# Two attentions and four experts on one core: one instruction for two heads' maxima, paired PSUM banks, rounded first layers

## The chip, the cores and the metric

The kernel runs on one core of a Trainium2 chip. The metric is the time of one execution on the device, in microseconds (us). TensorE multiplies matrices, VectorE, ScalarE and GpSimd work on vectors, SyncE starts the DMAs. Matrix results land in PSUM, eight banks of 512 float32 columns on 128 partitions; here ScalarE and VectorE empty them.

## The reference

The input x has 2048 tokens of width 128. All is float32.

```
x = x + attention1(layernorm(x))      # 16 heads of 64, position encoding added to the keys
x = x + block2(layernorm(x))
block2(s):
    a = attention2(s) @ Wo + bo       # 16 heads of 8, softmax over all 2048 keys
    x = layernorm(s + a) * g1 + b1
    key = floor(x @ router_w + router_b) mod 4
    for e in 0..3:  y_e = relu(x @ W1[e] + b1[e]) @ W2[e] + b2[e]    # 128 -> 512 -> 128
    return layernorm(x + y_key) * g2 + b2
```

Every softmax subtracts a maximum per query and head, as the kernel does too.

## The kernel before

Each engine has a program written out by hand; semaphores join them. The first attention has 32 chunks (8 pairs of heads, 4 chunks of 512 queries). A chunk has 8 double steps `j`, each with two key tiles of 128: scores on TensorE (three rounded products for each of two heads, L511), a seed with minus the maxima and an exponential on ScalarE (L842, L835), values (L533). The sums of the exponentials are added up on GpSimd and VectorE (L999, L1399, L1663).

The second attention has 16 blocks, each of 4 heads and 512 queries, of 16 steps each. A step has four score tiles of 512 columns on 32 rows of the array each (`scores2`, L639) in three banks in turn (`sc2`), four exponentials on ScalarE (`exps2`, L857), and the values (`values2`, L653, eight instructions for four heads). For a later block it also finds maxima: four matmuls (`max2`, L619) of 128 queries by 512 keys, one head each, and for each a VectorE instruction that takes the maximum of a row (`reduce_max`, L1480). TensorE's order in step T is:

```
scores2(T+1, 0); max2 of heads 2, 3; scores2(T+1, 1); values2(T)
scores2(T+2, 2); max2 of heads 0, 1; scores2(T+2, 3); items2(n, t)
```

The text calls the second line's scores and maxima group C, and those of the next step's first line, up to its values, group A. The maxima of group C are b, those of group A are a. From `MAX2_STEPS` = 11 on, a step's maxima are those of the block after next. An item (`items2`) is one further use of a bank: rows of the output (`o`, step 1), a query projection (`Q2`, step 3), the maxima's transposition (`fin2`, step 11), key and value projections in blocks 0 and 1, in blocks 4, 8 and 12 the end of the attention (`ot`, `wo`), the tokens' transposition (`xt`) and the router (`rk`). In the blocks after these, the steps of `FF_STEPS` hold the experts' work of the chunk before: first layers (`hidden`, L698, one float32 matmul, emptied by ScalarE with relu, L917) and second layers (`expert_out`, L706, added by VectorE, L1574). The last chunk's experts stand in the tail (`end2`).

All uses of a bank stand in one list, `USES`. A use waits with `begin` until the use before it on its bank is emptied:

```
BANK[n] = n % 3                  # up to the blocks
BANK[n] = four banks in turn     # in the blocks and the tail, the fourth from the scores' banks
pe.wait_ge(free[BANK[n]], NTH[n] - 1)
```

The maxima of block 0, and the first 28 tiles of block 1 (`EARLY_TILES`), are found before block 0. `tiles_late1` puts the first half of block 0's tiles into the last chunk of the first attention, two at each half of a double step; `start2` has the second half and four early tiles, and 24 early tiles stand between the first scores of block 0. `LATE1` says where the first projections of the second attention stand, and `late` where GpSimd splits them into a rounded part and a rest (`split2`).

Of the kernel before, what the change touches and what calls it, by code (L numbers as in the profile page):

```python
# [9 lines left out]
F32 = mybir.dt.float32  # L10
# [37 lines left out]
LOADS3 = 5 + 5 + 2 * E  # L48
# [34 lines left out]
def recip_quarters(j):  # L83
# [93 lines left out]
MAX2_STEPS = 11  # L177
KEYS2 = (0, 2, 1, 3)
SPLIT_BY_DVE = [("K2", 0, 3)]
EARLY2 = STEPS2 - MAX2_STEPS  # L180


def tiles2(n, t):

    to = n + 1 if t < MAX2_STEPS else n + 2
    q, kc = divmod((t + EARLY2) % STEPS2, NC)
    if to >= BLOCKS2:
        return [], []
    return [(to, h, q, kc) for h in (2, 3)], [(to, h, q, kc) for h in (0, 1)]
# [13 lines left out]
FF_STEPS = (2, 4, 5, 6, 7, 8, 9, 10, 12, 13, 14)  # L203


def items2(n, t):
# [3 lines left out]
    if n < 2:  # L210
        if n == 0 and t in (3, 6):
            items.append(("V2", {3: 2, 6: 3}[t]))
        if t in (5, 7, 8, 9):
            items.append(("K2", n + 2, (5, 7, 8, 9).index(t)))
# [6 lines left out]
    if c > 0:  # L221
        if g == 0:
            items += {5: [("ot", c - 1)], 7: [("wo", c - 1)], 14: [("xt", c - 1)], 15: [("rk", c - 1)]}.get(t, [])
        elif t in FF_STEPS:
            k = FF_STEPS.index(t) + len(FF_STEPS) * (g - 1)
# [11 lines left out]
EARLY_TILES = [("max2", 1, h, *divmod(i, NC)) for i in range(EARLY2) for h in (2, 3, 0, 1)]  # L237

# [11 lines left out]
def uses2():  # L250
    uses = []
    for n in range(BLOCKS2):
        for t in range(STEPS2):
            first, second = tiles2(n, t)
            uses += [("max2", *x) for x in first + second] + items2(n, t)
    return uses + end2()


USES_BEFORE = uses1() + start2() + EARLY_TILES[4:]
USES = USES_BEFORE + uses2()  # L260
# [4 lines left out]
FILLED = [0] * (RING + 1)  # L265
# [8 lines left out]
def build(nc, x, w_pairs, wout_pairs, bqk_pairs, bv_pairs, b_out, pos, wqk_groups, wv2, bqk_groups, bv2,  # L274
          parts, w_o, b_o, router_w, router_b, w1, b1, w2, b2, ln1_g, ln1_b, ln2_g, ln2_b, identity, out):
    ctx = ExitStack()
    with ctx:
# [32 lines left out]
        w1_sb = w_all[:].rearrange("p a n -> p (a n)")[:, 0:E * FF].rearrange("p (e n) -> p e n", e=E)  # L310
        o2 = accp[:].rearrange("p a b c -> p (a b c)").rearrange("p (t n) -> p t n", t=NT)
# [30 lines left out]
        w2_sb = sb("w2_sb", [128, E, FT, 128])  # L342
        own_sum = prob_flat[:, 0:QT * DM].rearrange("p (t n) -> p t n", t=QT)
        ff = sb("ff", [128, 2, QT, DM])
# [12 lines left out]
        sc = [ctx.enter_context(nc.psum_tensor(f"scores{h}", [128, 2, CW], F32)) for h in range(2)]  # L357
        acc_o = ctx.enter_context(nc.psum_tensor("acc_o", [128, CW], F32))
        ring = [ctx.enter_context(nc.psum_tensor(f"ring{n}", [128, CW], F32)) for n in range(RING)]
        ring = [bank[:] for bank in ring] + [sc[1][:, 1, :]]  # L360
        sc2 = [sc[0][:, 0, :], sc[0][:, 1, :], sc[1][:, 0, :]]
# [3 lines left out]
        full = [sem(f"full{b}") for b in range(RING + 1)]  # L365
        free = [sem(f"free{b}") for b in range(RING + 1)]
# [5 lines left out]
        seeded = sem("seeded")  # L372
        pool_acc, dve_acc = sem("pool_acc"), sem("dve_acc")
# [7 lines left out]
        ld2, w1_ld, ld3 = sem("ld2"), sem("w1_ld"), sem("ld3")  # L381
# [43 lines left out]
        def _(pe):  # L425
            def begin(key):
# [4 lines left out]
                elif BANK[n] == RING:  # L431
# [1365 lines left out]
```

## Time and profile before

| what | us |
|---|---|
| median of 3 runs | 2156.04 |
| these runs | 2151.03 to 2161.16 |
| the profiled execution, its own time | 2153.33 |
| its span, from first to last instruction | 2151.5 |

The first attention takes the first 1317 us or so of the span, the junction up to 1369.9, the blocks up to 2097 and the tail the rest. The profile marks, for each engine, when it was busy; matmuls overlap, and their ends are modelled, so that a start-to-start distance tells more of TensorE than a duration. A matmul's row has its operands, as `scores<-q_all,k_all`, and its rows and columns. PEclk is the TensorE clock granted in a stretch, as a share of 2.4 GHz. In a timeline, neighbours of one line are merged, with their count.

### The profile page before, as it was taken

Reading aid. Unit: us, or ns where it says so; the run is one execution under the profiler, and the core shown is the slowest. Engines: PE = TensorE matmul, PEld = TensorE weight load, DVE = VectorE, ACT = ScalarE, POOL = GpSimd, SP = SyncE. Lnnn points to the kernel's source line nnn. Section 1 sums busy time; section 2 is a strip of 40 time slices with the busy share of each in tenths; the row PEclk is TensorE's granted clock in tenths of the full one; section 3 lists DMA queues with packets and bytes.
Section 4 is the critical chain, followed back from the end, with each engine's and each line's share of the span. In section 5 each row is a group of like instructions: output and inputs, shape, how many; then the busy total and the mean of one; then the engine's idle time right before and its main releaser. Section 6 shows DMA issues by size and latency. Waiting matters only on the chain.

```text
span 2151.5 us, 35648 instructions
## 1 busy us (share of the span) xinstructions
PE 2069.2 (96%) x12010; PEld 929.7 (43%) x12010; DVE 1690.9 (79%) x2738; ACT 1704.3 (79%) x2298; POOL 1267.3 (59%) x763
## 2 busy tenths in 40 slices
PE   6999999999999999999999988999999999999997
PEld 3544444445444444454454433333333333333334
DVE  6677787777877878777877847789999999999803
ACT  1678888888888888888888884488888878888872
POOL 1578898897997988988988795331041033025003
PEclk7899999999999999999999998699999999999998
DMA  4000000000010000000000100000000000000000
GB/s 124 20 16 16 31 16 29 18 16 31 16 31 16 18 29 16 31 16 21 26 16 31 35 16 0 1 1 2 2 1 1 2 6 1 2 1 7 2 1 11
DMA packets 32038, 36.31 MB, mean 17 GB/s; under 512 B 12340, under 2 KB 23228, under 8 KB 31736
## 3 DMA queue, kind: packets, MB, share of 16 engines
q1 hardware_dynamic: 31864, 34.03, 5.1%
q8 instruction: 104, 1.70, 0.3%
q14 instruction: 70, 0.57, 0.1%
HBM read 32.46 MB, written 1.43 MB: 16 GB/s over the span
## 4 chain that ended last, share of the span: by engine, by line
PE 81%; ACT 7%; DVE 6%; issue 3%; POOL 2%; DMA 0%; DVEq 0%; ACTq 0%; POOLq 0%
PE acc_o L533 18%; PE scores L511 14%; PE acc_o L653 11%; PE scores L639 10%; PE ring L486 8%; ACT prob L835 3%; DVE mxp L1480 3%; ACT prob L857 2%; PE ring L698 2%; PE ring L619 2%; PE ring L706 2%; POOL accp L999 2%; PE ring L463 2%; PE ring L451 2%; PE ring L552 2%
## 5 line engine op out<-in xcount | busy, mean ns | idle before, releaser
L1363 DVE TENSOR_REDUCE mxp<-ring 128x1 f32<-128x512 f32 x1024 | 656.3, 684 | 232.5 <-PE ring L486 215.9
L999 POOL TENSOR_TENSOR accp<-accp,prob 128x1024 f32<-128x1024 f32 x318 | 799.4, 2514 | 55.0 <-ACT prob L835 11.4
L857 ACT ACTIVATE prob<-scores 128x512 f32<-128x512 f32 x1024 | 543.9, 599 | 138.0 <-PE scores L639 135.7
L835 ACT ACTIVATE prob<-scores 128x1024 f32<-128x1024 f32 x512 | 519.4, 1015 | 149.4 <-PE scores L511 130.1
L1480 DVE TENSOR_REDUCE mxp<-ring 128x1 f32<-128x512 f32 x789 | 510.8, 684 | 54.7 <-PE ring L619 39.1
L511 PE MATMUL scores<-q_all,k_all 64*128 64x512 f32 x3072 | 545.5, 408 | 7.3 <-ACT scores L842 4.9
L842 ACT ACTIVATE scores<-minus_all 128x1024 f32<-128x1024 f32 x510 | 524.4, 1028 | 24.1 <-ACT prob L835 0.8
L533 PE MATMUL acc_o<-prob,v 128*64 128x512 f32 x2048 | 499.6, 608 | 2.9 <-ACT v L817 2.9
L486 PE MATMUL ring<-k_all,q_all 64*128 64x512 f32 x1024 | 394.4, 432 | 10.3 <-DVE mxp L1363 5.3
L511 PEld LDWEIGHTS scores<-q_all,k_all 64*128 64x128 f32 x3072 | 335.9, 186 | 83.7 <-ACT scores L842 40.9
L639 PE MATMUL scores<-q_all,k_all 32*128 32x512 f32 x1024 | 304.9, 495 | 13.0 <-ACT prob L857 8.8
L486 PEld LDWEIGHTS ring<-k_all,q_all 64*128 64x128 f32 x1024 | 190.4, 188 | 249.7 <-issue 232.1
L619 PE MATMUL ring<-k_all,q_all 32*128 32x512 f32 x789 | 286.5, 504 | 8.3 <-DVE mxp L1480 4.0
L653 PE MATMUL acc_o<-prob,v 128*16 128x512 f32 x2048 | 274.0, 607 | 0.2 <-ACT prob L857 0.2
L639 PEld LDWEIGHTS scores<-q_all,k_all 32*128 32x128 f32 x1024 | 118.1, 184 | 331.5 <-ACT prob L857 306.5
L1045 POOL TENSOR_SCALAR rounded<-kf,parts_sb 128x512 fp32r<-128x512 f32 x31 | 49.5, 1597 | 347.7 <-ACT kf L885 347.7
L533 PEld LDWEIGHTS acc_o<-prob,v 128*64 128x64 f32 x2048 | 129.5, 137 | 246.9 <-issue 194.6
L1399 DVE TENSOR_TENSOR accp<-accp,prob 128x1024 f32<-128x1024 f32 x124 | 211.7, 1707 | 19.6 <-POOL accp L999 19.6
L996 POOL TENSOR_TENSOR accp<-prob 128x1024 f32<-128x1024 f32 x32 | 103.2, 3223 | 143.6 <-ACT prob L835 143.6
L1480 DVE TENSOR_REDUCE mxp<-scores 128x1 f32<-128x512 f32 x235 | 160.8, 684 | 9.8 <-PE scores L619 4.5
L619 PEld LDWEIGHTS ring<-k_all,q_all 32*128 32x128 f32 x789 | 113.9, 188 | 58.6 <-issue 57.0
L1028 POOL TENSOR_SCALAR lnv<-mv 128x4 f32<-128x4 f32 x10 | 4.2, 422 | 225.1 <-DVE mv L1458 113.5
(187 smaller groups left out, 1523.3 us busy)
## 6 DMA issues: line engine op xcount, KB each, us to landing
minus_all<-m_dram SPq DMA_DIRECT2D x32, 512.0 KB, 3.6
rec<-rec_dram SPq DMA_DIRECT2D x60, 128.0 KB, 2.9
w_all<-w_pairs SPq DMA_DIRECT2D x1, 1344.0 KB, 11.2
x<-x SPq DMA_DIRECT2D x4, 256.0 KB, 3.8
pos_sb<-pos SPq DMA_DIRECT2D x1, 1024.0 KB, 7.0
w_sb<-w SPq DMA_DIRECT2D x4, 256.0 KB, 4.6
w_all<-w SPq DMA_DIRECT2D x1, 1024.0 KB, 5.7
q_all<-m_rows SPq DMA_DIRECT2D x64, 2.0 KB
```

The lines of the kernel that those rows point to most:

```text
L486: end(nc.tensor.matmul(bank[:], qhi[half(h), c, q * 128:(q + 1) * 128], khi[half(h), p % 2, kc * CW:(kc + 1) * CW], start=True, stop=True) ...
L511: last = nc.tensor.matmul(sc[u][:, h, :], of_k[half(h), p % 2, of_keys], of_q[half(h), c, :], start=(n == 0 and not seeded1(T)), stop=(n = ...
L533: last = nc.tensor.matmul(acc_o[half(h), :], v1[:, p % 2, t, half(h)], prob[:, T % SLOTS1, h, :], start=(t == 0), stop=(t == NT - 1))
L619: end(nc.tensor.matmul(bank[:], q_all[quarter(h), n % 4, q * 128:(q + 1) * 128], k_all[quarter(h), KEYS2[n % GROUPS], kc * CW:(kc + 1) * C ...
L639: nc.tensor.matmul(sc2[place % 3], k_all[quarter(h), KEYS2[n % GROUPS], t * 128:(t + 1) * 128], q_all[quarter(h), n % 4, :], start=True, s ...
L653: last = nc.tensor.matmul(acc_o[32 * h:32 * h + VW, :], v2[:, t, 4 * (n % GROUPS) + h, :], prob2[:, h // 2, T % 2, h % 2, :], start=(t == ...
L835: nc.scalar.activation(prob[:, T % SLOTS1, :, :], sc[T % 2][:, :, :], ACT.Exp, scale=SCALE1).then_inc(exp_done, 1)
L842: nc.scalar.activation(sc[T % 2][:, :, :], minus_all[:, T // NT % 2], ACT.Copy).then_inc(seeded, 1)
L857: nc.scalar.activation(prob2[:, h // 2, T % 2, h % 2, :], sc2[place % 3], ACT.Exp, scale=SCALE2).then_inc(exp2_done, 1)
L999: nc.gpsimd.tensor_tensor(accp[:, k % 2], accp[:, k % 2], prob[:, T % SLOTS1], ALU.add).then_inc(pool_acc, 1)
L1363: done(nc.vector.reduce_max(mxp1[k % 2][:, h * QT + q, kc:kc + 1], bank[:], AX.X), ("max", k, q, kc, h))
L1480: done(nc.vector.reduce_max(mxp2[n % 2][:, h * QT + q, kc:kc + 1], bank[:], AX.X), key)
```

## The change

- Maxima in the blocks: `pair2` puts two heads' tiles into two adjacent banks, and one `reduce_max` of 2 x 512 columns empties both. A step has two pairs where it had four tiles.
- Banks: PSUM is one tensor. In the blocks all uses, items too, take in turn one of two pairs of banks (3 and 4, 5 and 6; an item uses the first of its pair). In the tail, seven single banks take turns.
- Experts' first layers: weights and tokens are split into a rounded part and a rest (`split_w1` and `split_x` on GpSimd, for the last chunk ScalarE and VectorE), and three rounded matmuls replace one float32 matmul.
- Last chunk of the first attention: three tiles at each half of a double step in place of two, 16 of the early tiles among them; the rest of the early tiles stand in `start2`, and none between the first scores. The tiles run over the queries first.
- Second query projection: from the last chunk to the end of the one before. Value and key projections in block 0: to steps 0 and 1, and 2, 3, 5, 7.
- Experts' items: 12 in block 14 and 9 in block 15, in place of 11 and 10.
- The second weights are loaded after the first attention, into its maxima's place.

```diff
@@ order of the work
-         (CHUNKS1 - 2, 6): [("K2", 1, 0)],
+         (CHUNKS1 - 2, 6): [("K2", 1, 0)], (CHUNKS1 - 2, 7): [("Q2", 1)],
...
-         (CHUNKS1 - 1, 3): [("Q2", 1)], (CHUNKS1 - 1, 5): [("K2", 1, 1)], (CHUNKS1 - 1, 6): [("T2", 2)],
+         (CHUNKS1 - 1, 5): [("K2", 1, 1)], (CHUNKS1 - 1, 6): [("T2", 2)],
...
-    tiles = [("max2", 0, h, q, kc) for kc in range(2) for q in range(QT) for h in (2, 3, 0, 1)]
+    first, second = ([("max2", 0, h, q, kc) for q in range(QT) for h in (2, 3, 0, 1)] for kc in range(2))
+    tiles = first + EARLY_TILES[:16] + second
     n = 2 * j + half
-    return tiles[2 * n:2 * n + 2]
+    return tiles[3 * n:3 * n + 3]
...
+    if k == LAST1:
+        return [], tiles[:3], tiles[3:]
     return tiles[:1], tiles[1:3], tiles[3:]
...
-    return [(to, h, q, kc) for h in (2, 3)], [(to, h, q, kc) for h in (0, 1)]
+    return [("pair2", to, h, q, kc) for h in (2, 0)]
...
 FF_STEPS = (2, 4, 5, 6, 7, 8, 9, 10, 12, 13, 14)
+FF_ENDS = {BLOCKS2 - 2: (2, 4, 5, 6, 7, 8, 9, 10, 12, 13, 14, 15), BLOCKS2 - 1: (0, 2, 3, 5, 6, 8, 10, 12, 14)}
...
-            + [("fin2", 0), ("K2", 1, 3)] + EARLY_TILES[:4])
+            + [("fin2", 0), ("K2", 1, 3)] + EARLY_TILES[16:])
@@ banks
-BANK = [n % RING if n < len(USES_BEFORE) else (RING, *((len(USES_BEFORE) + b) % RING for b in range(RING)))[(n - len(USES_BEFORE)) % (RING + 1)]
-        for n in range(len(USES))]
+PAIR = RING
+SINGLE = RING + 2
+BANK = ([n % RING for n in range(len(USES_BEFORE))] + [PAIR + n % 2 for n in range(len(USES_BLOCKS))]
+        + [SINGLE + n % 7 for n in range(len(end2()))])
...
+        pairs = [psum[:, 3:5, :], psum[:, 5:7, :]]
+        ring = [psum[:, b, :] for b in (4, 5, 6, 3, 5, 3, 4, 5, 6, 0, 1, 2)]
@@ TensorE
+            def pair2(n, h0, q, kc):
...
+                begin(key)
+                for a in range(2):
+                    h = h0 + a
+                    last = nc.tensor.matmul(pairs[bank_of(key) - PAIR][:, a, :], q_all[quarter(h), n % 4, q * 128:(q + 1) * 128],
+                                            k_all[quarter(h), KEYS2[n % GROUPS], kc * CW:(kc + 1) * CW], start=True, stop=True)
+                end(last, key)
...
-                end(nc.tensor.matmul(bank[:], w1_sb[:, e, f * 128:(f + 1) * 128], xnt[:, c * CW:(c + 1) * CW],
-                                     start=True, stop=True), ("h", c, e, f))
+                cols = slice(f * 128, (f + 1) * 128)
+                for n, (w, tokens) in enumerate(((w1hi, x2hi), (w1hi, x2lo), (w1lo, x2hi))):
+                    last = nc.tensor.matmul(bank[:], w[:, e, cols], tokens[:, c % 2, :], start=(n == 0), stop=(n == 2))
+                end(last, ("h", c, e, f))
@@ ScalarE, the last chunk's tokens
+                elif kind == "xt" and it[1] == NC - 1:
...
+                    nc.scalar.activation(x2hi[:, it[1] % 2, :], bank[:], ACT.Copy).then_inc(tail_hi, 1)
+                    act.wait_ge(tail_lo, 1)
+                    copy_side(it, xnt[:, it[1] * CW:(it[1] + 1) * CW], bank[:])
@@ GpSimd
+            def split_w1():
...
+                for e in range(E):
+                    nc.gpsimd.tensor_tensor(w1hi[:, e, :], w1_sb[:, e, :], zero[:].to_broadcast([128, FF]), ALU.subtract).then_inc(w1_hi, 1)
+                    pool.wait_ge(w1_hi, e + 1)
+                    nc.gpsimd.tensor_tensor(w1lo[:, e, :], w1_sb[:, e, :], w1hi[:, e, :].bitcast(F32), ALU.subtract).then_inc(w1_lo, 1)
...
-                    if t == 7 and k == LAST1:
-                        late(k, 3)
...
+                    late(k, 7)
@@ VectorE
+            def pair2(n, h0, q, kc):
+                key = ("pair2", n, h0, q, kc)
+                wait_full(dve, key)
+                to = mxp2[n % 2].rearrange("p (h t) c -> p h t c", h=4)
+                done(nc.vector.reduce_max(to[:, h0:h0 + 2, q, kc], pairs[bank_of(key) - PAIR], AX.X), key)
```

## Rows read from the trace of the kernel before

**Rows 1.** The page's head: span, and each engine's busy time, share and instructions

```profile
span 2151.5 us, 35648 instructions
...
PE 2069.2 (96%) x12010; PEld 929.7 (43%) x12010; DVE 1690.9 (79%) x2738; ACT 1704.3 (79%) x2298; POOL 1267.3 (59%) x763
```

**Rows 2.** Stretches: length; busy PE, PEld, DVE, ACT, POOL; clock; DMA share, GB/s

```profile
1369.90:1388.50 18.60, 17.84 (x82) 5.45 (x80) 11.33 (x19) 9.70 (x19) 0.70 (x1) 0.50 0.00 1
1388.50:1423.60 35.10, 34.25 (x211) 11.42 (x211) 29.72 (x49) 28.03 (x55) 14.29 (x10) 1.00 0.00 1
...
1511.10:1553.60 42.50, 40.80 (x264) 13.64 (x263) 40.48 (x69) 34.31 (x68) 2.86 (x2) 1.00 0.01 2
1553.60:1598.10 44.50, 42.64 (x288) 16.12 (x287) 42.12 (x79) 35.65 (x69) 10.59 (x14) 1.00 0.01 1
...
1644.10:1690.10 46.00, 45.27 (x322) 17.52 (x321) 42.75 (x75) 38.10 (x73) 2.85 (x2) 1.00 0.01 2
```

**Rows 3.** Timeline of TensorE, plain steps of block 3: start, duration, line, operands, count

```profile
1527.18 1.05 PE L653 MATMUL acc_o<-prob,v 128*16 128x512 f32 x8
1528.16 0.50 PE L639 MATMUL scores<-q_all,k_all 32*128 32x512 f32 x1
...
1529.77 1.05 PE L653 MATMUL acc_o<-prob,v 128*16 128x512 f32 x8
```

**Rows 4.** Timeline of TensorE, block 15, which has no maxima

```profile
2064.40 1.05 PE L653 MATMUL acc_o<-prob,v 128*16 128x512 f32 x8
...
2066.99 1.05 PE L653 MATMUL acc_o<-prob,v 128*16 128x512 f32 x8
```

**Rows 5.** Timeline of VectorE in the junction, early tiles

```profile
1360.61 9.66 DVE L1480 TENSOR_REDUCE mxp<-ring 128x1 f32<-128x512 f32 x16 [0.36 <-PE ring L619]
```

**Rows 6.** Timeline of TensorE, two steps of block 6 with an item each

```profile
1656.82 1.13 PE L698 MATMUL ring<-xnt,w_all 128*128 128x512 f32 x2
1657.88 0.50 PE L639 MATMUL scores<-q_all,k_all 32*128 32x512 f32 x1
...
1659.30 0.50 PE L639 MATMUL scores<-q_all,k_all 32*128 32x512 f32 x1
...
1659.74 1.16 PE L706 MATMUL ring<-w_sb,prob 128*128 128x128 f32 x8
1660.83 0.50 PE L639 MATMUL scores<-q_all,k_all 32*128 32x512 f32 x1
...
1662.24 0.50 PE L639 MATMUL scores<-q_all,k_all 32*128 32x512 f32 x1
```

**Rows 7.** Groups by line and shape in the blocks: busy, mean ns; idle before

```profile
L857 ACT ACTIVATE prob<-scores 128x512 f32<-128x512 f32 x908 | 481.8, 599 | 109.0 <-PE scores L639 106.9
L1480 DVE TENSOR_REDUCE mxp<-ring 128x1 f32<-128x512 f32 x681 | 442.6, 684 | 30.2 <-PE ring L619 15.1
...
L1488 DVE TENSOR_REDUCE mx<-mxp 128x16 f32<-128x64 f32 x14 | 3.1, 221 | 2.1 <-DVE mxp L1480 2.1
```

**Rows 8.** Timeline of VectorE, the same stretch of block 6

```profile
1659.87 0.69 DVE L1480 TENSOR_REDUCE mxp<-scores 128x1 f32<-128x512 f32 x1
```

**Rows 9.** Timelines of VectorE and TensorE, a release in the last chunk

```profile
1315.68 2.47 DVE L1480 TENSOR_REDUCE mxp<-ring 128x1 f32<-128x512 f32 x4
...
1316.51 0.48 PE L619 MATMUL ring<-k_all,q_all 32*128 32x512 f32 x1 [0.69 <-DVE mxp L1480]
```

**Rows 10.** Timeline of TensorE, last chunk of the first attention

```profile
1296.51 0.50 PE L619 MATMUL ring<-k_all,q_all 32*128 32x512 f32 x1
1296.94 0.96 PE L511 MATMUL scores<-q_all,k_all 64*128 64x512 f32 x6
1297.83 0.50 PE L619 MATMUL ring<-k_all,q_all 32*128 32x512 f32 x2
```

**Rows 11.** Timeline of TensorE, two first layers in the tail

```profile
2120.99 1.02 PE L698 MATMUL ring<-xnt,w_all 128*128 128x512 f32 x2
...
2122.74 0.59 PE L698 MATMUL ring<-xnt,w_all 128*128 128x512 f32 x1
```

More of the change, by code:

```diff
@@ L47 @@
 LOADS2 = 4
-LOADS3 = 5 + 5 + 2 * E
+LOADS3 = 5 + 5 + E
 RING = 3
@@ L210, in items2 @@
     if n < 2:
[L211 to L214, printed above, removed]
+        if n == 0 and t < 2:
+            items.append(("V2", 2 + t))
+        steps = (2, 3, 5, 7) if n == 0 else (5, 7, 8, 9)
+        if t in steps:
+            items.append(("K2", n + 2, steps.index(t)))
     if t == 1 and n > 0:
@@ L223, in items2 @@
             items += {5: [("ot", c - 1)], 7: [("wo", c - 1)], 14: [("xt", c - 1)], 15: [("rk", c - 1)]}.get(t, [])
-        elif t in FF_STEPS:
-            k = FF_STEPS.index(t) + len(FF_STEPS) * (g - 1)
+        elif t in ff_steps(n):
+            k = ff_steps(n).index(t) + sum(len(ff_steps(b)) for b in range(GROUPS * c + 1, n))
             items += experts(c - 1)[k:k + 1]
@@ L253, in uses2 @@
         for t in range(STEPS2):
[L254 to L260, printed above, removed]
-USE = {key: n for n, key in enumerate(USES)}
-BANK = [n % RING if n < len(USES_BEFORE) else (RING, *((len(USES_BEFORE) + b) % RING for b in range(RING)))[(n - len(USES_BEFORE)) % (RING + 1)]
-        for n in range(len(USES))]
-FILLED = [0] * (RING + 1)
+            uses += tiles2(n, t) + items2(n, t)
+    return uses
+USES_BEFORE = uses1() + start2()
+USES_BLOCKS = uses2()
+USES = USES_BEFORE + USES_BLOCKS + end2()
+USE = {key: n for n, key in enumerate(USES)}
+PAIR = RING
+SINGLE = RING + 2
+BANK = ([n % RING for n in range(len(USES_BEFORE))] + [PAIR + n % 2 for n in range(len(USES_BLOCKS))]
+        + [SINGLE + n % 7 for n in range(len(end2()))])
+FILLED = [0] * (SINGLE + 7)
 NTH = []
@@ L355, in build @@
         mask = sb("mask", [128, E, NT])
[L357 to L361, printed above, removed]
+        psum = ctx.enter_context(nc.psum_tensor("psum", [128, 8, CW], F32))
+        sc = [psum[:, 0:2, :], psum[:, 2:4, :]]
+        acc_o = psum[:, 7, :]
+        sc2 = [psum[:, b, :] for b in range(3)]
+        pairs = [psum[:, 3:5, :], psum[:, 5:7, :]]
+        ring = [psum[:, b, :] for b in (4, 5, 6, 3, 5, 3, 4, 5, 6, 0, 1, 2)]
         x_ld, ident_ld, pos_ld = [sem(f"x_ld{c}") for c in range(NC)], sem("ident_ld"), sem("pos_ld")
         pair0_dma, pairs_dma = sem("pair0_dma"), sem("pairs_dma")
-        full = [sem(f"full{b}") for b in range(RING + 1)]
-        free = [sem(f"free{b}") for b in range(RING + 1)]
+        full = [sem(f"full{b}") for b in range(SINGLE + 7)]
+        free = [sem(f"free{b}") for b in range(SINGLE + 7)]
         tokens_ready = sem("tokens_ready")
@@ L786, in _ @@
                     T = STEPS2 * n + t
-                    first, second = tiles2(n, t)
+                    tiles = tiles2(n, t)
                     scores2(T + 1, 0)
-                    for x in first:
-                        max2(*x)
+                    for it in tiles[:1]:
+                        pair2(*it[1:])
                     scores2(T + 1, 1)
@@ L793, in _ @@
                     scores2(T + 2, 2)
-                    for x in second:
-                        max2(*x)
+                    for it in tiles[1:]:
+                        pair2(*it[1:])
                     scores2(T + 2, 3)
@@ L1202, in _ @@
                         normalised4(c - 2)
+                    if n == 2 and t == 5:
+                        split_w1()
                     for it in items2(n, t):
@@ L1285, in _ @@
                     sp.dma_start(w1_sb, w1.rearrange("e k n -> k e n")).then_inc(w1_ld, 16)
+            sp.wait_ge(exp_done, NT * CHUNKS1)
+            for e in range(E):
+                sp.dma_start(w2_sb[:, e], w2[e].rearrange("(f k) n -> k f n", k=128)).then_inc(w2_ld, 16)
             out_t = out.rearrange("(t p) n -> p t n", p=128)
@@ L1715, in _ @@
                         mred2(n + 1)
-                    for u, couple2 in enumerate(tiles2(n, t)):
-                        for x in couple2:
-                            max2(*x)
+                    tiles = tiles2(n, t)
+                    for u in range(2):
+                        for it in tiles[u:u + 1]:
+                            pair2(*it[1:])
                         if n >= GROUPS and n % GROUPS == 0 and t in (8, 9):
```

77 lines of the change are left out of this document (55 added, 22 removed).

## The prediction

> **What bounds the kernel now.** I read the page's head first [rows 1], to see how full each engine is. TensorE is marked busy for 96%, and VectorE and ScalarE for 79% each: that alone doesn't say which of the three sets the pace. The busy times by stretch [rows 2] show where each is full: in a block with experts' work (1644.1 to 1690.1) TensorE 45.3 of 46.0 us and VectorE 42.8, in one without (1511.1 to 1553.6) 40.8 and 40.5 of 42.5. The stretches were cut at the values matmuls that open a block of 16 steps. The change relieves VectorE, so the question is whether a step waits for it.
>
> The order of instructions settles that. In a plain step TensorE starts the values at 1527.18, opens the next group of scores and maxima matmuls 0.98 us later, at 1528.16, and the next values come at 1529.77 [rows 3]. That is 2.59 us a step. In block 15 there are no maxima at all, and two values groups are again 2.59 us apart [rows 4]: the step is a circle of TensorE and ScalarE over three score banks, and the four maxima instructions (pitch 0.60 us where they run back to back: 16 in 9.66 us [rows 5]; 2.4 us a step) just fit beneath it. In a step with an item (a projection, a transposition or an expert's matmuls) TensorE's own list is the limit: group C at 1659.30, item at 1659.74, group A at 1660.83, next C at 1662.24, so 0.44 + 1.09 + 1.41 = 2.94 us [rows 6]. VectorE isn't waited for there either.
>
> **The blocks' maxima.** Two 512-column instructions of 684 ns become one of 1024 columns. Between 64 and 512 columns the time grows from 221 to 684 ns, or 1.03 ns a column [rows 7], so the pair takes 0.684 + 512 x 1.03 ns = 1.21 us, against a pitch of 2 x 0.60 before. VectorE gains about 0.1 us a step, and by the plain step that gain is worth nothing: what it shortens is already hidden beneath the circle.
>
> What the change takes away is banks. The old ring gives four single banks in turn; the new one has two pairs, and *every* use, an item too, takes a whole pair. In a plain step the uses are a, b, a, b: pair b waits for the b before it. An item shifts the turn: a, b, item, a. The a after an item stands on the pair that b used in the same step. So group A, and the score and the values queued behind it on TensorE, wait until VectorE has reduced b. From the start of C: matmul to reduction 0.57 us (1659.30 to 1659.87 [rows 6, 8]); reduction 1.21; release of the bank to TensorE's next matmul 0.15 (one reduction starts at 1315.68 and lasts 0.68, and the matmul that waited for it starts at 1316.51 [rows 9]). Group A thus can't start before 1.93 us, where it now starts at 1.49 to 1.53. Then 1.41 us to the next C [rows 6]: **3.34 us for each step with an item**, whichever item it is, against 2.91 to 2.94. ScalarE doesn't lengthen this: four exponentials and an item's copy at about 0.60 each are 3.0 us [rows 7]. VectorE has 2.42 us of pairs and at most one short addition, also less. The item itself waits for the previous a, which is free again about 0.5 us into the step, so it isn't late.
>
> How many steps: a block with experts' work has an item after each of steps 1 to 14. Its 46.0 us are 14 s + 2 x 2.59, so s = 2.91 now [rows 2], and each costs 0.43 more. Blocks 5, 6, 7, 9, 10, 11, 13 have 98 of them: **+42 us**. Blocks 4, 8 and 12 have 7 each; 44.5 us are 7 s + 9 x 2.59, s = 3.03 [rows 2], +0.31 x 21 = **+6.5**; block 1 is like them, **+2**. Blocks 2 and 3 have 3 each, s = 2.94 from 42.5 us, +0.40 x 6 = **+2.4**. Block 14 has 8 steps with a further pair behind the item, **+3.5**. Together **+56 us**. The two unknowns are the pair's duration and the release. The pair can't well be under two pitches less one fixed part (1.20 - 0.15, from the intercept of the same two rows), nor over two separate instructions (1.37); the release lies between 0.05 and 0.15, of which I take the measured one. That makes a step 3.08 to 3.50 us, and over the 148 steps the sum +18 to +80.
>
> **Experts' first layers, rounded.** One full-precision matmul (1656.82 to 1657.88, 1.06 us with the change of tiling behind it [rows 6]) becomes three rounded ones. The nearest rows are the three rounded pairs of a score tile in the first attention: 1296.94 to 1297.83, 0.89 us [rows 10]. It saves 0.17 us in itself. In the blocks with maxima the saving is nothing, since group A waits for the bank anyway; it would be 48 x 0.17 = 8 us with that cover gone. In block 15 and the tail it counts. The tail now runs at 1.75 us per pair of one first-layer and one second-layer item, all TensorE [rows 11]; 12 of these at about 0.2 less are 2.5 us, and the first four, which run at half clock, bring twice 0.2 each, 1.7. The last chunk's split adds one VectorE instruction of some 0.7 us (a maxima instruction is the nearest row [rows 7]) between the copy and the first layer. Items of block 15 give 1 us. Seven banks at the end save nothing, as no bank is waited for there. Together **-4 us** (0 to -6). The Trainium skill, FP8 and Floating Point Precision, TensorE Precision Notes, counts a true FP32 matmul as four passes; three rounded ones would by that save a quarter of it, an estimate of 0.26 us in place of the 0.17, or about 1 us more in the tail.
>
> GpSimd gets the weights' split, eight instructions in block 2. A block of this kind has two such on GpSimd now, in 2.9 of 42.5 us [rows 2]; eight are some 12 us, while it is idle. It also gets a token split of two per chunk (3 us), while it waits for the router. It delays the router by at most a microsecond; nothing. The second weights' four loads move to the end of the first attention, five blocks before their first use: nothing.
>
> **Tiles in threes, in the last chunk of the first attention.** Now each of its eight double steps has tile groups of 1, 2 and 1, each 0.43 us of TensorE with its change of tiling [rows 10]. They become two groups of three. One group less saves 0.43. But three tiles fill the three banks, and the second group needs the first one's: reductions start 0.53 us after the first group and take 0.60 each, so its third tile starts at 0.53 + 2 x 0.60 + 0.68 + 0.15 = 2.56 us, where TensorE is there after 0.43 + 0.89 = 1.32. So 1.24 is lost and 0.43 saved: +0.8 us in each of eight. At the end VectorE's additions, which the last sums wait for, stand behind two more tiles (+1.2), part of the rest lies beneath other waits. I take **+6 us** (bounds: -3 if the banks never bind, +10 if every wait adds). The second query projection moves to the end of chunk 30: TensorE does it 1.06 us earlier, ScalarE's copy of it waits for the key split on GpSimd, and the chunk's additions on GpSimd start some 3 us later, which its idle time in that chunk takes up. Nothing, or +1.
>
> **The junction.** 16 of 28 tiles leave the stretch where VectorE is full (16 in 9.66 us [rows 5]). That is 9.6 us. But the first six scores and their exponentials now lie beneath those tiles and will stand alone behind them. A group of scores at half clock is 0.8 us, five exponentials one behind another are 3.0, group A and the bank turns between them about 2 more, and the last tiles' own way through the ring 1.5 to 2: some 7.5 us are given back. **-2 us**. Block 0 takes 53.7 us, its first 18.6 at a granted clock of 0.50, that is 1.2 GHz [rows 2]. The full-array value and key projections move to its first steps. The clock rose at 1388.5, in the step after the first such projection, so it may rise sooner; the steps behind items cost 3.34 here too. **-2 us** (0 to -5).
>
> **The sum.** +56 - 4 + 6 - 2 - 2 = +54 us, made against the profiled execution: 2151.5 us of span [rows 1], 2153.3 in its own time. That gives **2207 us**. This execution lies 2.7 us below the median of 2156.0, well within the runs' 2151 to 2161.
>
> **Rivals.** (a) *The bank's wait is hidden*: group A starts when TensorE gets there, as now. This would need matmul start, reduction and release in under 1.49 us, a pair of at most 0.77 us. Then first layers save their 8 us, and -8 - 4 + 6 - 2 - 2 = -10 gives 2143, faster by 0.6%. For it speaks only that no such pair is in the trace; against it the slope of 1.03 ns a column. Chance 0.10. (b) *VectorE is the limit after all*, since it is over 90% busy in the blocks. Each of some 230 steps then gets 0.13 us shorter, -30 on top of (a): 2113. Block 15's 2.59 us without maxima speaks against it. Chance 0.03. The Trainium skill, TensorEngine Tiling (Array Packing), PSUM Bottleneck, says that after row tiling the copy out of PSUM may become the bottleneck and should be vectorised over several tiles; by that rule this rival would hold. (c) *The waits add up*: the idle 0.4 us in each step lets the clock fall in some blocks, as it does where TensorE waits at the junction; the plain steps of block 3, in which TensorE waits for ScalarE, ran at granted clock 1.00 [rows 2], so that is unlikely. One to two blocks at half speed cost 15 to 30 us more: about 2230. Chance 0.08. (d) Pair and release both at their lower bound: 2169, the main case's thin end.
>
> **Chances and range.** The main case has 0.76, with its own range 2178 to 2226. With (c) and the costlier bounds the range becomes 2172 to 2234, which leaves out (a), (b) and thin ends, about 2 in 10. A change of under 0.5% (11 us) can hardly be told from none. Faster 0.12, same 0.04, slower 0.84.
>
> **What would show it.** Pair reductions of 1.2 us; steps behind an item at 3.3 us and plain ones at 2.59; idle time of TensorE before the maxima's pair matmuls, ended by VectorE, of some 0.4 us and over 100 times; blocks with experts' work of 52 us in place of 46. The last chunk's double steps at 5.8 us. If steps behind an item stay at 2.9 or fall, the bank argument is wrong, and with it the forecast's sign. If reductions last much longer or shorter than 1.2 us, only the size is.

## The result and the profile after

The changed kernel takes 2213.72 us (median of 5 runs, 2210.95 to 2235.77), the one before 2156.04 beside it (5 runs, 2151.03 to 2161.16). The ratio is 1.0283, 95% interval 1.0251 to 1.0315: slower by 2.8%, or 58 us. The forecast was 2207, slower. Of all runs of all kernels here one fell far out: an execution of the version with all but pairs and threes took 6498 us at a mean granted clock of 0.43; no ratio uses it, and that version's median is 2142.39 without it.

The profiled execution is the longest of the five, 2235.77 us. Its head, in the columns of [rows 1]:

```profile
span 2234.0 us, 34908 instructions
...
PE 2124.4 (95%) x12074; PEld 968.3 (43%) x12074; DVE 1668.2 (75%) x2269; ACT 1704.3 (76%) x2299; POOL 1281.3 (57%) x777
```

TensorE is marked busy for 95% against 96%. Its share hardly falls, and its busy time even grows by 55 us. The stretches, as in [rows 2], show where the time is: block 3, block 4, block 6.

```profile
1517.20:1561.10 43.90, 40.07 (x264) 13.63 (x263) 38.85 (x37) 34.56 (x68) 2.85 (x2) 1.00 0.01 1
1561.10:1614.20 53.10, 49.26 (x292) 17.64 (x295) 40.93 (x47) 36.12 (x69) 13.20 (x18) 0.84 0.00 1
1667.80:1720.30 52.50, 50.22 (x330) 20.86 (x331) 41.49 (x44) 38.03 (x73) 2.86 (x2) 1.00 0.01 1
```

Block 6 takes 52.5 us at full clock, where it took 46.0. VectorE is busy for 41.5 of them: relieved, and idle for 11. Block 4 is longer by 8.6, at a granted clock of 0.84. A second profile of the changed kernel, from a run of 2216 us, has block 4 at full clock:

```profile
1556.90:1604.20 47.30, 43.09 (x288) 15.95 (x287) 40.89 (x47) 36.27 (x70) 13.25 (x18) 1.00 0.00 1
...
1964.70:2017.70 53.00, 49.25 (x288) 17.58 (x287) 41.83 (x55) 36.16 (x69) 20.90 (x30) 0.84 0.02 6
```

There block 12 (the second line) is the slow one. So block 4 has two terms: 2.8 us of waits, and 5.8 that belong to the clock.

A step with an item, TensorE's timeline of block 6 in the profile after; it answers to [rows 6]:

```profile
1673.35 0.50 PE L655 MATMUL psum<-k_all,q_all 32*128 32x512 f32 x2 [0.42 <-DVE mxp L1553]
...
1674.76 0.50 PE L675 MATMUL psum<-q_all,k_all 32*128 32x512 f32 x1
...
1675.26 1.13 PE L748 MATMUL psum<-minus_all,prob 128*128 128x128 f32 x8
1676.32 0.50 PE L675 MATMUL psum<-q_all,k_all 32*128 32x512 f32 x1
1676.71 0.49 PE L655 MATMUL psum<-k_all,q_all 32*128 32x512 f32 x2
...
1677.14 1.05 PE L689 MATMUL psum<-prob,v 128*16 128x512 f32 x8
1678.12 0.50 PE L675 MATMUL psum<-q_all,k_all 32*128 32x512 f32 x1
```

and VectorE's, in the same steps:

```profile
1675.34 1.23 DVE L1553 TENSOR_REDUCE mxp<-psum 128x2 f32<-128x1024 f32 x1 [0.23 <-PE psum L655]
1676.48 0.34 DVE L1646 SCALAR_TENSOR_TENSOR w_all<-psum,mask,w_all 128x128 f32<-128x128 f32 x1
1677.24 1.23 DVE L1553 TENSOR_REDUCE mxp<-psum 128x2 f32<-128x1024 f32 x1 [0.42 <-PE psum L655]
```

Group C opens at 1674.76, its reduction starts 0.58 later and ends at 1676.57, and group A's pair, on the same two banks, starts at 1676.71, 0.14 after that. The next C comes 1.41 later, at 1678.12: 3.36 us. The score ahead of the pair (1676.32) gets out on time; the values behind it don't. Of 0.39 us of waiting no idle mark is left, since the modelled end of the waiting score (1676.82) lies over it. Only where the item is a short one, at 1673.35, is a wait marked. The groups of the whole kernel say the same, as in [rows 7]:

```profile
L1553 DVE TENSOR_REDUCE mxp<-psum 128x2 f32<-128x1024 f32 x470 | 568.0, 1224 | 154.0 <-PE psum L655 153.4
...
L655 PE MATMUL psum<-k_all,q_all 32*128 32x512 f32 x940 | 239.3, 507 | 19.7 <-DVE mxp L1553 15.1
```

TensorE shows 15.1 us of idle time behind the reductions, for a loss of four times as much; VectorE waits 153 us for TensorE, which waits for VectorE. Starts tell it, idle marks don't.

### The profile page after: what moved, and what is told of

Its sections match the earlier page's. It is cut to its first block and busy times, and to the rows that moved or that the text cites. A ratio compares the mean times of both kernels' runs of the same rounds, so it can differ in the third digit from the quotient of the medians.

```text
span 2234.0 us, 34908 instructions
## 1 busy us (share of the span) xinstructions
PE 2124.4 (95%) x12074; PEld 968.3 (43%) x12074; DVE 1668.2 (75%) x2269; ACT 1704.3 (76%) x2299; POOL 1281.3 (57%) x777
## 5 line engine op out<-in xcount | busy, mean ns | idle before, releaser
L1430 DVE TENSOR_REDUCE mxp<-psum 128x1 f32<-128x512 f32 x1024 | 656.4, 684 | 232.5 <-PE psum L511 215.4
L895 ACT ACTIVATE prob<-psum 128x512 f32<-128x512 f32 x1024 | 547.3, 600 | 203.2 <-PE psum L675 201.8
L1553 DVE TENSOR_REDUCE mxp<-psum 128x2 f32<-128x1024 f32 x470 | 568.0, 1224 | 154.0 <-PE psum L655 153.4
L873 ACT ACTIVATE prob<-psum 128x1024 f32<-128x1024 f32 x512 | 519.4, 1014 | 150.6 <-PE psum L536 131.5
L536 PE MATMUL psum<-q_all,k_all 64*128 64x512 f32 x3072 | 545.5, 408 | 7.3 <-ACT psum L880 4.9
L880 ACT ACTIVATE psum<-minus_all 128x1024 f32<-128x1024 f32 x510 | 524.4, 1028 | 24.1 <-ACT prob L873 0.8
L558 PE MATMUL psum<-prob,v 128*64 128x512 f32 x2048 | 502.2, 611 | 2.9 <-ACT v L855 2.9
L511 PE MATMUL psum<-k_all,q_all 64*128 64x512 f32 x1024 | 394.1, 432 | 10.3 <-DVE mxp L1430 5.3
L675 PE MATMUL psum<-q_all,k_all 32*128 32x512 f32 x1024 | 357.8, 507 | 20.6 <-ACT prob L895 20.3
L536 PEld LDWEIGHTS psum<-q_all,k_all 64*128 64x128 f32 x3072 | 336.4, 186 | 86.9 <-ACT psum L880 42.1
L655 PE MATMUL psum<-k_all,q_all 32*128 32x512 f32 x940 | 239.3, 507 | 19.7 <-DVE mxp L1553 15.1
```

What stands on the lines that cost most here:

```text
L511: end(nc.tensor.matmul(bank[:], qhi[half(h), c, q * 128:(q + 1) * 128], khi[half(h), p % 2, kc * CW:(kc + 1) * CW], start=True, stop=True) ...
L536: last = nc.tensor.matmul(sc[u][:, h, :], of_k[half(h), p % 2, of_keys], of_q[half(h), c, :], start=(n == 0 and not seeded1(T)), stop=(n = ...
L558: last = nc.tensor.matmul(acc_o[half(h), :], v1[:, p % 2, t, half(h)], prob[:, T % SLOTS1, h, :], start=(t == 0), stop=(t == NT - 1))
L655: last = nc.tensor.matmul(pairs[bank_of(key) - PAIR][:, a, :], q_all[quarter(h), n % 4, q * 128:(q + 1) * 128], k_all[quarter(h), KEYS2[n ...
L675: nc.tensor.matmul(sc2[place % 3], k_all[quarter(h), KEYS2[n % GROUPS], t * 128:(t + 1) * 128], q_all[quarter(h), n % 4, :], start=True, s ...
L873: nc.scalar.activation(prob[:, T % SLOTS1, :, :], sc[T % 2][:, :, :], ACT.Exp, scale=SCALE1).then_inc(exp_done, 1)
```

## The experiments

All kernels were compared with runs of the kernel before on their chip. Its median there was 2155.4 (19 runs) beside the first four, 2153.2 (21) beside the next four and 2157.0 (7) beside the last.

**Single tiles.** The changed kernel with single tiles and four single banks in the blocks.

```diff
-    return [("pair2", to, h, q, kc) for h in (2, 0)]
+    return [("max2", to, h, q, kc) for h in (2, 3, 0, 1)]
...
-BANK = ([n % RING for n in range(len(USES_BEFORE))] + [PAIR + n % 2 for n in range(len(USES_BLOCKS))]
+BANK = ([n % RING for n in range(len(USES_BEFORE))] + [PAIR + n % 4 for n in range(len(USES_BLOCKS))]
```

> The changed kernel with one part undone: in the blocks, the maxima are again four single tiles with one reduction each, and all uses take four single banks in turn; all else is as changed. Theory of the bank turn: group A no longer waits for a pair, so steps with an item fall from 3.36 us to TensorE's own list, 2.94 us with a second layer and about 2.74 with a rounded first layer (2.91 less 0.17); plain steps stay at 2.59. The time falls by 60 to 75 us from 2213.7, to about 2148 us. Rival, the cost lies in other parts (rounded first layers, GpSimd's splits, the clock's falls): blocks with experts' work stay above 50 us and the kernel above 2190.

Measured: 2147.48 us (10 runs), ratio 0.9970 (0.9952 to 0.9988). Without the pairs, and with all else of the change, the kernel is a little faster than before. Undoing the pairs gives back 66 us. In blocks 1 to 15 no stretch at half clock is left in its profile. Steps with a second layer are 2.94 again, those with a rounded first layer 2.81, not 2.74.

**Pairs alone.** The kernel before, with pairs of banks and `pair2`; first layers, junction and last chunk as before.

```diff
-    return [(to, h, q, kc) for h in (2, 3)], [(to, h, q, kc) for h in (0, 1)]
+    return [("pair2", to, h, q, kc) for h in (2, 0)]
...
+        pairs = [psum[:, 3:5, :], psum[:, 5:7, :]]
```

> The kernel before with one part of the change alone: two heads' maxima in two adjacent banks with one reduction, and two pairs of banks in turn for all uses of the blocks; float32 first layers, four single banks in the tail, junction as before. Theory of the bank turn: steps with an item go to 3.36 us whatever the item is, so the float32 first layer costs nothing more; 148 steps times 0.43 is 64 us in the profile's terms, about 2215 us in all. Rival, the pairs alone cost little and the rounded layers or the splits are needed for the loss: under 2175.

Measured: 2217.38 us (4 runs), ratio 1.0316 (1.0266 to 1.0365). The whole loss comes with the pairs alone; whether it is a little more, the interval doesn't tell. Steps behind an item are 3.36 or 3.37 us, a first layer in full precision too; the steps with the maxima's transposition in blocks 4, 8 and 12 are longer (3.66 to 3.68), and a few others are 3.42 to 3.45. Both sides of the ablation agree.

**A short reduction.** The changed kernel, where the reduction reads 64 of the 512 columns of each bank: seven eighths of the keys are left out of the maxima.

```diff
-done(nc.vector.reduce_max(to[:, h0:h0 + 2, q, kc], pairs[bank_of(key) - PAIR], AX.X), key)
+done(nc.vector.reduce_max(to[:, h0:h0 + 2, q, kc], pairs[bank_of(key) - PAIR][:, :, 0:64], AX.X), key)
```

> The changed kernel, whose pair reduction reads only the first 64 columns of each of the two banks (so the maxima subtracted are those of a part of the keys; nothing else is left out). The matmuls, the pairs and their turn are unchanged, only the time VectorE holds a pair falls from 1.22 to some 0.25 us. Theory of the bank turn: the wait for a pair ends before TensorE gets there, so steps with an item fall to 2.94 and 2.74 us and plain ones stay at 2.59; about 2148 us, as with single tiles. Rival 1, VectorE is the limit of the plain steps too: they fall below 2.5 us and the kernel below 2120. Rival 2, two matmuls on one semaphore and adjacent banks cost by themselves: the steps stay at 3.3 us and the kernel above 2200.

Measured: 2132.96 us (4 runs), ratio 0.9905 (0.9876 to 0.9933). With the same two places in turn, but each held for less time, the loss is gone, so it isn't the order of the uses by itself. And it is 14.5 us under the kernel with single tiles, which I hadn't expected. Timeline of VectorE in block 6, this kernel:

```profile
1650.55 0.29 DVE L1553 TENSOR_REDUCE mxp<-psum 128x2 f32<-128x128 f32 x1 [1.13 <-PE psum L655]
1651.87 0.29 DVE L1553 TENSOR_REDUCE mxp<-psum 128x2 f32<-128x128 f32 x1 [1.02 <-PE psum L655]
```

and in the same block of the kernel with single tiles:

```profile
1647.08 3.88 DVE L1546 TENSOR_REDUCE mxp<-psum 128x1 f32<-128x512 f32 x6 [0.22 <-PE psum L643]
1650.87 0.25 DVE L1576 RECIPROCAL rs<-psum 128x16 f32<-128x16 f32 x1
1651.15 0.29 DVE L1578 TENSOR_TENSOR accp<-psum,rs 128x128 f32<-128x128 f32 x1
1651.36 2.47 DVE L1546 TENSOR_REDUCE mxp<-psum 128x1 f32<-128x512 f32 x4
```

VectorE there works without a gap from 1647.08 to 1653.83. The step with the rows of the output (0.6 us on TensorE) falls from 2.81 to 2.59 when reductions are short, one with a first layer from 2.81 to 2.75, the one with the maxima's transposition from 2.81 to 3.44 down to 2.59. Second layers stay at 2.94 and plain steps at 2.59, but for one plain step in each of blocks 4, 8 and 12, ahead of that transposition, which falls from 3.03 to 2.60. So VectorE's pace does count in steps whose item is short for TensorE, and where VectorE has more to do than the maxima; in the other plain steps and beside second layers it doesn't.

**Threes alone.** The kernel before, with the last chunk's tiles in threes, the early tiles among them, and the second query projection moved.

```diff
-    return tiles[2 * n:2 * n + 2]
+    return tiles[3 * n:3 * n + 3]
...
-USES_BEFORE = uses1() + start2() + EARLY_TILES[4:]
+USES_BEFORE = uses1() + start2()
```

> The kernel before with the junction's part alone: tiles in threes and 16 early tiles in the last chunk of the first attention, the rest of the early tiles ahead of the first scores, the second query projection one chunk earlier, tiles over queries first. Theory: the second group of three waits for the first one's banks, so the last chunk gets longer by 11 us (as the changed kernel's trace has it), the junction shorter by 5; together +4 to +8 us, about 2162. Rival, the shorter junction also brings the full clock sooner in block 0: a net gain, under 2153.

Measured: 2159.15 us (10 runs) where 2162 was expected, ratio 1.0019 (0.9999 to 1.0038): a small loss at most, which the runs don't surely tell from none. Its profile has 20.5 us at half clock in block 15 (49.4 in place of 42.2 us), where the kernel before has 3.4; this one execution owes 7 us to that.

**Rounded first layers alone.** The kernel before, with only the first layers rounded.

```diff
-                end(nc.tensor.matmul(bank[:], w1_sb[:, e, f * 128:(f + 1) * 128], xnt[:, c * CW:(c + 1) * CW],
-                                     start=True, stop=True), ("h", c, e, f))
+                for n, (w, tokens) in enumerate(((w1hi, x2hi), (w1hi, x2lo), (w1lo, x2hi))):
+                    last = nc.tensor.matmul(bank[:], w[:, e, cols], tokens[:, c % 2, :], start=(n == 0), stop=(n == 2))
```

> The kernel before with the experts' first layers rounded (and the splits they need), and nothing else of the change. Theory: TensorE's list is the limit in steps with an item, so steps with a first layer go from 2.91 to 2.81 us as in the kernel with single tiles, blocks with experts' work from 46.0 to 45.4, and block 15 and the tail give about 2: 7 x 0.5 + 2 = 5 to 6 us, 2150, ratio 0.997 to 0.998. Rival, a product saved is worth 0.17 us in each of 64 first layers: 11 us, 2145. Rival, the splits on GpSimd and ahead of the tail delay as much as is saved: 2155 to 2157.

Measured: 2145.72 us (12 runs), ratio 0.9960 (0.9943 to 0.9977), 7.5 us faster. That lies between the expected 5 to 6 and the rival's 11, and the interval holds both. Its profile decides: 4.2 come from blocks 1 to 14 (627.2 for 631.4), where the rival's 0.17 in each of 48 first layers would be 8, 1.9 from block 15 and 2.3 from the tail, and steps with a first layer are 2.81 us.

**All but pairs and threes.** The single-tile kernel with last chunk and junction as before; rounded first layers, the moved items of block 0 and of blocks 14 and 15 and the seven banks remain.

```diff
-    return tiles[3 * n:3 * n + 3]
+    return tiles[2 * n:2 * n + 2]
...
-USES_BEFORE = uses1() + start2()
+USES_BEFORE = uses1() + start2() + EARLY_TILES[4:]
```

> The kernel with single tiles in the blocks, and the first attention's last chunk and the junction as they were: tiles in twos, early tiles between the first scores. What is left of the change are the rounded first layers, the items moved in block 0 and in blocks 14 and 15, and seven banks in the tail. Theory: threes cost about 4 us by the run with the threes alone (2159.2 against 2155.4), so 2147.5 less 4 is 2143 to 2144, ratio 0.994 to 0.995. Rival, the threes only moved time from the junction into the chunk and cost nothing: 2147 to 2148.

Measured: 2142.63 us (10 runs), ratio 0.9944 (0.9926 to 0.9962). This is the best version that leaves nothing out, faster than both kernels. Its junction and block 0, as stretches:

```profile
1317.00:1370.30 53.30, 47.34 (x108) 20.94 (x107) 42.02 (x74) 9.21 (x17) 22.14 (x27) 0.58 0.01 3
1370.30:1418.10 47.80, 46.88 (x288) 15.78 (x287) 41.03 (x67) 37.67 (x73) 15.00 (x11) 0.97 0.00 1
```

Block 0 takes 47.8 us where it took 53.7 [rows 2]: full clock from 1372.8 on, where it was 1388.5. Against the kernel with rounded layers alone (53.5) that is 5.8 us, by the moved projections or by the clock that comes back earlier; no run tells these two apart. The clock's return isn't set by the moved items alone: the kernel with pairs alone has everything ahead of block 0 and the projections as before, and in its profile full clock is back at 1377.9. By the medians the two kernels are 3.1 us apart, since block 15 and the tail are 1.8 longer here and blocks 1 to 14 0.4. The threes, which cost this version 4.8 us (two series on two chips), leave less of it: block 0 is 49.1 with them, and the start of block 0 comes 6 us later.

**Three quarters.** The changed kernel, where the reduction reads 384 columns of each bank: a quarter of the keys is left out.

```diff
-done(nc.vector.reduce_max(to[:, h0:h0 + 2, q, kc], pairs[bank_of(key) - PAIR], AX.X), key)
+done(nc.vector.reduce_max(to[:, h0:h0 + 2, q, kc], pairs[bank_of(key) - PAIR][:, :, 0:384], AX.X), key)
```

> The changed kernel, where the reduction over a pair of banks reads 384 of the 512 columns of each (a quarter of the keys is left out of the maxima). Theory: the step behind an item is C to reduction, reduction, release and the rest of TensorE's list, so it follows the reduction's length one for one: 256 columns less at 1.03 to 1.05 ns make 0.96 us in place of 1.22, the step 3.10 in place of 3.36, and 148 such steps give 38 us: 2213.7 less 38 is 2176, ratio 1.008 to 1.011. Rival, the loss is that items and pairs share two places at all, whatever the length: above 2205. Rival, TensorE's list is the limit from here down: 2150.

Measured: 2174.21 us (4 runs), ratio 1.0094 (1.0066 to 1.0121). The theory said 2176. The steps are 3.10 us, as TensorE's timeline of block 6 shows:

```profile
1658.62 0.49 PE L675 MATMUL psum<-q_all,k_all 32*128 32x512 f32 x1
...
1660.14 0.50 PE L675 MATMUL psum<-q_all,k_all 32*128 32x512 f32 x1
1660.29 0.49 PE L655 MATMUL psum<-k_all,q_all 32*128 32x512 f32 x2
...
1661.70 0.50 PE L675 MATMUL psum<-q_all,k_all 32*128 32x512 f32 x1
```

and VectorE's:

```profile
1659.19 0.96 DVE L1553 TENSOR_REDUCE mxp<-psum 128x2 f32<-128x768 f32 x1 [0.49 <-PE psum L655]
```

VectorE's reduction starts at 1659.19 and ends at 1660.15; the pair follows 0.14 later. That is 0.57 + 0.96 + 0.14 + 1.41 = 3.08, the same sum with one term changed. The rival in which the length didn't matter is out.

**The changed kernel again.** No edit.

> The changed kernel once more, for a second profile. Theory: time 2211 to 2215 in most runs. The three stretches at half clock at the ends of blocks 4, 8 and 12 in the first profile, which was 22 us above the median, are an accident of that execution: here none or one of them, with the same steps of 3.36 and 2.59 us elsewhere, and blocks 4, 8 and 12 of about 50 us. Rival, they belong to the kernel: then they come again at the same places, and the median holds them.

Measured: 2216.41 us (4 runs, 2212.81 to 2230.97), ratio 1.0302. One stretch at half clock in the blocks, 2000.4 to 2020.9, at the end of block 12, and the same steps elsewhere; undisturbed, blocks 4 and 8 take 47.3 us, not about 50. So neither theory held in full: the stretches keep to the same places (first profile: 1596.7, 1808.3 and 2019.9, the ends of blocks 4, 8 and 12), but which of the three come differs from run to run.

**Pairs, two reductions.** The changed kernel with its pairs of banks, each emptied by two instructions.

```diff
-done(nc.vector.reduce_max(to[:, h0:h0 + 2, q, kc], pairs[bank_of(key) - PAIR], AX.X), key)
+both = pairs[bank_of(key) - PAIR]
+nc.vector.reduce_max(to[:, h0:h0 + 1, q, kc], both[:, 0, :], AX.X)
+done(nc.vector.reduce_max(to[:, h0 + 1:h0 + 2, q, kc], both[:, 1, :], AX.X), key)
```

> The changed kernel with its pairs of banks, where each pair is emptied by two instructions of 512 columns, one behind the other, in place of one of 1024. It tells the joined instruction from the pairing of banks. Theory: a use keeps the pair from the matmul to the end of the second reduction, 0.60 + 0.68 = 1.28 us in place of 1.22, so the steps behind an item are 3.42 in place of 3.36, 148 x 0.06 = 9 us more, about 2222, ratio 1.032 to 1.035; all of the loss is the pairing, and joining the two instructions gives back only these 9. Rival, the joined instruction is the loss (one long reading of two banks): steps of 2.81 to 2.95, about 2150. Rival, VectorE's start of the second instruction hides behind the first by more than that: 2213 to 2216.

Measured: 2231.50 us (4 runs, 2223.15 to 2237.98), ratio 1.0357 (1.0316 to 1.0398). The interval reaches over the expected 1.032 to 1.035; the profiled run took 2225.56. VectorE's timeline:

```profile
1676.59 0.69 DVE L1554 TENSOR_REDUCE mxp<-psum 128x1 f32<-128x512 f32 x1 [0.16 <-PE psum L655]
1677.20 0.68 DVE L1555 TENSOR_REDUCE mxp<-psum 128x1 f32<-128x512 f32 x1
```

From 1676.59 to 1677.88 is 1.29 us, and the steps are 3.42 us, as expected. The joined instruction isn't the culprit: it is the one part of the pairing that gives something back, 0.06 us a step. The loss is that two tiles share one place and are released together; no run frees the first bank of a pair ahead of the second, so these two aren't told apart. The median lies 9 us above the expected 2222, and I have no profile of those longer runs; their granted clock was 0.962 and 0.966 against 0.970 and 0.972 in the two shorter, which fits more stretches at half clock.

## Why the prediction was right, and where it was off

The sign, the mechanism and nearly the size held. That 2207 came so near 2213.72 is partly luck: the last chunks cost 3 to 5 us more than forecast and the junction gave 3 to 4 more back. In the table the stretches are cut at first values matmuls, as in the forecast; us against the profiled execution before.

| term | forecast | first profile | second profile |
|---|---|---|---|
| blocks 1 to 14 at full clock | +56 | +59.6 | +59.6 |
| their stretches at half clock | 0 (rival c) | +22.5 | +7.0 |
| chunks 30 and 31 | +6 | +11.1 | +9.1 |
| junction | -2 | -5.0 | -6.1 |
| block 0 | -2 | -3.3 | -2.3 |
| block 15 | -1 | -1.5 | -1.4 |
| tail | -3 | -1.0 | -0.9 |
| before chunk 30 | 0 | 0.0 | -2.1 |
| sum | +54 | +82.4 | +62.9 |

The first line takes blocks 4, 8 and the ones behind them from the second profile, where they are undisturbed; blocks 12 and 13 are disturbed in both, and are put at 47.30 and 52.50, as blocks 8 and 10 are there (47.06 + 43.82 + 43.86 + 47.26 + 52.58 + 52.46 + 51.61 + 47.30 + 52.40 + 52.44 + 51.58 + 47.30 + 52.50 + 48.80 = 690.97, before 631.40); the second is the rest of these blocks.

**The item step.** Forecast 0.57 + 1.21 + 0.15 + 1.41 = 3.34, measured 0.58 + 1.23 + 0.14 + 1.41 = 3.36. A slope over two rows of one operation, the shorter one reading SBUF, priced a shape that the trace didn't have to 0.014 us (1.224 measured). "VectorE gains about 0.1 us a step" doesn't follow from 1.21 against 1.20; two pair reductions back to back take 2.33 to 2.35 us, a pitch of some 1.11, so it gains 0.2. It was rightly priced at nothing in plain steps. By groups of blocks: the seven with experts' work +44.1 (forecast 42), blocks 4, 8, 12 +7.5 (6.5), block 1 +2.1 (2), blocks 2 and 3 +2.6 (2.4), block 14 +3.4 (3.5). Three experiments hold it up: the step follows the reduction's length down (3.10 at 384 columns), follows it up (3.42 with two reductions), and vanishes with single banks. Rival (a) is out, and (b) as the limit of this kernel: its VectorE is idle for a fifth of block 6. Of what the prediction named as signs, one was wrong: the idle time of TensorE before the pair matmuls, "of some 0.4 us and over 100 times". The wait is there, its mark mostly isn't. "So it isn't late", said of the item, holds in most steps, but not in step 11 of blocks 4, 8 and 12, which takes 3.66 to 3.68 us.

**Rival (c) came in part.** I gave stretches at half clock 0.08 in place of the main case; in fact they are added to it in some executions. Each cost 7 to 8 us. One begins like this, TensorE at the end of block 4 in the first profile:

```profile
1594.80 0.27 PE L662 MATMUL psum<-ident,mx 128*16 128x128 f32 x1 [0.62 <-DVE mxp L1553]
...
1595.93 0.50 PE L655 MATMUL psum<-k_all,q_all 32*128 32x512 f32 x2 [0.44 <-DVE mxp L1553]
...
1596.36 1.64 PE L689 MATMUL psum<-prob,v 128*16 128x512 f32 x8
...
1599.41 0.79 PE L675 MATMUL psum<-q_all,k_all 32*128 32x512 f32 x1 [0.25 <-ACT prob L895]
...
1604.16 1.91 PE L689 MATMUL psum<-prob,v 128*16 128x512 f32 x8
```

The step before took 3.68 us, the longest of the block at full clock: its item, the maxima's transposition (1594.80), waits 0.62 us for a reduction too. Then the clock falls, and scores take 0.79 for 0.50 and values 1.91 for 1.05. My ground against (c), plain steps at full clock in block 3, didn't bear on it: what differs here is a longer step, not many short waits. That this wait brings the fall is argued from its place (in the four profiles with full pairs there are six falls in blocks 1 to 13, five of them in step 12 of block 4, 8 or 12 and a short one at 1610.7; in the profiles of the other kernels, the one before too, there is none), not shown. The place alone isn't enough: those four profiles have 12 such steps, of 3.66 to 3.90 us, and 7 of them, the three longest among these, have no fall right behind them. The four other runs, at 2211 to 2214 us, have mean clocks of 0.971 to 0.979 as against 0.957, which fits fewer of them than in the profiled one.

**The last chunk**, the term that was most mis-sized: +11.1 and +9.1 for +6, above my upper bound of +10 in one case. The query projection moved into chunk 30 lengthens its last double step from 4.94 to 6.78 us, where I said nothing or +1. Of chunk 31's seven double steps between first and last values four grew by 0.73 to 0.79 in the second profile, as the sum of 1.24 - 0.43 said, and one fell by 0.17. The first two grew by 1.9 and 2.4, for another reason. (Named as a sign were double steps of 5.8 us: the last five are 5.7 to 6.9 in that profile and 6.4 to 7.8 in the first.) TensorE and VectorE at these first two, in the second profile:

```profile
1276.04 0.50 PE L644 MATMUL psum<-k_all,q_all 32*128 32x512 f32 x3
...
1277.41 1.66 PE L644 MATMUL psum<-k_all,q_all 32*128 32x512 f32 x3
1282.02 1.97 PE L570 MATMUL psum<-accp,ones 128*64 128x512 f32 x4 [2.95 <-DVE accp L1466]
1283.78 3.49 PE L558 MATMUL psum<-prob,v 128*64 128x512 f32 x8
```

```profile
1276.57 3.68 DVE L1547 TENSOR_REDUCE mxp<-psum 128x1 f32<-128x512 f32 x6 [0.95 <-PE psum L644]
1280.17 1.80 DVE L1466 TENSOR_TENSOR accp<-accp,prob 128x1024 f32<-128x1024 f32 x1
```

VectorE does six reductions ahead of the addition that the sums wait for. TensorE waits 2.95 us (2.66 before), the clock falls to half in this wait (at 1280.2), and the sums take 1.97 (before 1.08) and the values 3.49 (before 1.89): 2.5 us of clock that no term held. I had the wait for the addition, at the end, as +1.2, and not what it did to the clock. All seven profiles with threes have this fall. It isn't theirs alone: the kernel with pairs alone and the best version keep this chunk as it was, wait 2.7 us there, and fall too, for 3.4 us and at a cost of 1.6 to 1.7, while the kernel before and the one with rounded layers alone don't fall.

**The junction**, forecast -2, measured -5.0 and -6.1: 9.6 us of tiles leave it as said, but what comes back is 3.5 to 4.6, not 7.5. In the second profile VectorE ends the last early tiles at 1367.52, the exponentials start at 1367.46, beneath them, and the first values follow at 1370.79, 3.3 us later. I had priced scores, exponentials and bank turns one behind another; they overlap.

**First layers.** The pair of one first and one second layer in the tail, [rows 11] before, now from the profile after:

```profile
2204.99 0.71 PE L739 MATMUL psum<-q_all,w1hi 128*128 128x512 f32 x2
2205.54 0.39 PE L739 MATMUL psum<-q_all,w1lo 128*128 128x512 f32 x1
2205.77 1.05 PE L748 MATMUL psum<-minus_all,prob 128*128 128x128 f32 x8
2206.58 0.72 PE L739 MATMUL psum<-q_all,w1hi 128*128 128x512 f32 x2
```

It takes 1.59 us where it took 1.75: 0.16, against 0.17 in the forecast. The 0.26 estimated from the four passes in the Trainium skill, FP8 and Floating Point Precision, TensorE Precision Notes, isn't borne out here. The tail gains only 1.0 for 3 all the same: its half clock lasts until 2204.3, 23.8 us behind the last values, before until 21.9 us behind them. The kernel with rounded layers alone, whose clock comes back 21.1 us behind them, gains 2.3. "In the blocks with maxima the saving is nothing" was right beside pairs. With that cover gone it is 4 us, not the 8 that I named, since VectorE holds those steps at 2.81.

**VectorE.** "VectorE isn't waited for there either" was right of nearly all plain steps and of second layers, and wrong of steps with the shortest items (rows of the output, the maxima's transposition): in the kernel before they are 2.81 to 3.45 and would be 2.59 by TensorE. It changed nothing in the forecast, as its sum took each block's measured time.

## What to carry to other kernels

Count the places of a ring, not its bytes: merging two results into one place halves the turns, and each place is held for the sum of both readings. Here four places of 0.7 us of reading each were enough to hide the waits for a bank and two of 1.2 were not, as soon as a third use came between. Before an engine is relieved, find a step that waits for it; and once two terms of a step's loop are known from the trace (fill to reader, reader to next fill), the price of a merge is one line of arithmetic.

Take a bundle apart: the pairs cost 66 us and the threes 5, while the rounded first layers gave 7.5 and the moved items with the tail's banks 3 more.

## What was not expected of the hardware

- At equal work the same kernel took 2211 to 2236 us. The profiles differ by stretches of 20.5 to 23.9 us at half of TensorE's clock, at the ends of blocks 4, 8 and 12 when they come, 211.6 us apart in the first profile.
- The clock in the junction falls and comes back at places that the code doesn't fix. Before, its last fall there was at 1347.6 and it came back at 1388.5; with pairs alone, where all ahead of block 0 is the same, it was at half from 1330.2 to 1377.9; in the best version, with the first attention unchanged too, it fell at 1328.4, after a short fall at 1318.2, and came back at 1372.8. The time of the junction was much the same before and in the best version (53.0 and 53.3 us), and block 0 gained 5.9.
- One reduction over two adjacent banks took 1224 ns for 1024 columns, 957 for 768 and 292 for 128, one over a single bank 684 for 512: the three lie on one straight line of 1.04 ns a column, which passes 7 ns above the single bank's, so the second bank costs next to nothing extra.
